# Matmuls on a tile of ones at the start of a cross-attention and gated feed-forward kernel

## The chip, the core and the metric

One core of one Trainium2 chip runs the whole kernel. Five engines work side by side, each through a queue of its own: TensorE (PE) multiplies, VectorE (DVE), ScalarE (ACT) and GpSimd (POOL) do the rest of the arithmetic, and SyncE (SP) issues most DMAs. The metric is device time in microseconds of the whole program; lower is better.

## The reference

The computation is one gated block: cross-attention to a context, then a feed-forward with 4-bit weights. There are 16 batch elements, each with 128 channels and 512 positions, 8 heads of 16 channels, half of them rotated.

```python
def _L0_xattn_ref(x, c, Wq, bq, Wk, bk, Wv, bv, Wo, bo):
    q, k, v = _proj(Wq, bq, x), _proj(Wk, bk, c), _proj(Wv, bv, c)
    # each: (b, 8 heads, 512 positions, 16 channels); rope on the first 8 channels of q and k
    scores = jnp.einsum('bhqd,bhkd->bhqk', q, k) / jnp.sqrt(jnp.float32(kc))
    p_attn = jax.nn.softmax(scores, axis=-1)
    out = jnp.einsum('bhqk,bhkd->bhqd', p_attn, v)
    return _proj(Wo, bo, out)
def _L0_ffn_ref(x, ...):
    gate_up = jnp.einsum('bsh,oh->bso', x, w_gu)      # w_gu, w_down unpacked from 4 bits, scaled
    h = jax.nn.silu(gate) * up
    y = jnp.einsum('bsi,hi->bsh', h, w_down)
    return y / rms
x = x + jnp.tanh(g_xattn[0]) * _L0_xattn_ref(_layernorm(x), ctx_2048, ...)
x = x + jnp.tanh(g_ffn[0]) * _L0_ffn_ref(_layernorm(x), ...)
```

## The kernel before

The kernel is written with queues in an order set by hand: each engine has one list of instructions, and semaphores make it wait for the others. The first part (about 400 us) is the attention over 16 batch elements, the second the feed-forward in four groups.

Batch element `n` goes through these steps. DVE (from `n` = 3 on POOL) normalises its input to `xn`. PE projects q and k, in two halves of the channels, `project_rot` (L788) and `project_pass` (L794), each four instructions. ACT adds the bias (L946). DVE for `n` = 0 and POOL for the others rotate the result and split it into a rounded head and a rest, SP (and ACT once) stores both to an image in DRAM, and SP loads the image back as `qk_stack` in another layout (`load_first` for `n` = 0, `load_half` for the others). Then come the scores. A batch element has 16 slots; `score` (L815) multiplies two heads of one tile of queries into one of two PSUM banks `s_ps`, and DVE takes the maximum of each row out of that bank (`maxima`, L1119). A score waits for the maximum of the score two before it, since the bank is then free. After the eighth and the sixteenth slot `turn_max` (three small DVE operations) turns the maxima, which go through DRAM into two more rows of `qk_stack`. With these rows `weigh` (L827) multiplies the scores again, transposed, ACT takes the exponential, and `values` (L845) multiplies by v.

Batch elements overlap: `tensor_step(b)` has in each slot a score of `b + 1`, the weights of `b`, and the values of `b` from three slots before. In slots 2 and 3 it also has the two halves of the projection of `b + 3`. Ahead of `tensor_step(0)` stands the start of the program: nine matmuls on a tile of ones (`WARM`, L910), the projections of batch elements 0, 1 and 2, and then the 16 scores of batch element 0, with `project_v` (L800) behind slot 3 and two tiny products (L924, L928) behind slots 5 and 6. The image of batch element 0 must be stored and loaded between the projections and these scores.

The change sits in this start, in PE's queue (the function under `@block.tensor`). `v_ones` are the two halves of `v_all`, which DVE fills with ones at the program's start; the later values of v are written into part of them. `pv_ps` is the PSUM bank of the values, `st_ps` are three banks for projections and weights in turn.

Of the kernel before, what the change touches and what calls it, by code (L numbers as in the profile page):

```python
# [17 lines left out]
P = 128  # L18
# [29 lines left out]
ST_BANKS, S_BANKS = 3, 2  # L48
# [4 lines left out]
IMG_ROWS, K_ROW0 = 102, 49  # L53
GROUPS = B // GROUP
FIRST_TURN, TAIL_AT, WARM = 12, 3, 9
BANKS = 4
NT = (B // GROUP) * IT
LAG = 2
# [5 lines left out]
def score_of(slot):  # L64
    return slot // KT, slot % KT
# [8 lines left out]
def transposed_items():  # L74
    items = []
    for n in range(AHEAD_PROJ):
        items += [("rot", n), ("pass", n)]
    items.append(("v", 0))
    for b in range(B):
        for slot in range(SLOTS):  # L80
            if slot == V_AT and b + 1 < B:
                items.append(("v", b + 1))
            items += [("weight", b, 2 * slot), ("weight", b, 2 * slot + 1)]
            if slot == ROT_AT and b + AHEAD_PROJ < B:
                items.append(("rot", b + AHEAD_PROJ))
            if slot == PASS_AT and b + AHEAD_PROJ < B:
                items.append(("pass", b + AHEAD_PROJ))
            if slot == MIX_AT and b >= 2:
                items.append(("mix", b - 2))
    items += [("mix", B - 2), ("mix", B - 1)]  # L90
    return items
# [6 lines left out]
ST_NO = {item: n for n, item in enumerate(transposed_items())}  # L98
# [3 lines left out]
def feed_forward(nc, ctx, d, keep, tiles):  # L102
# [58 lines left out]
    def take_up(dve, T_, k):  # L161
        g, t = divmod(T_, IT)
        at = 4 * T_ + k
        dve.wait_ge(up_done, at + 1)
        bank, out, scale = gu_ps[(2 * k + 1) % BANKS], up[T_ % 2], gu_sc[:, k, IT + t:IT + t + 1]
        if k == 0:
# [146 lines left out]
    def take_gate(act, T_, k):  # L313
        at = 4 * T_ + k
        act.wait_ge(gate_done, at + 1)
        if T_ >= 2:
            act.wait_ge(pairs_ok, 2 * (T_ - 2) + 2)
        nc.scalar.activation(parts[T_ % 2][:, k], gu_ps[(2 * k) % BANKS], ACT.Copy,  # L318
                             scale=gu_sc[:, k, T_ % IT:T_ % IT + 1]).then_inc(gate_read, 1)
# [70 lines left out]
    def gate_up(pe, T_, n):  # L390
# [12 lines left out]
        for moving, first in ((x_head, True), (x_rest, False)):  # L403
            last = nc.tensor.matmul(gu_ps[n % BANKS], gu_vals[:, k, col:col + P], moving[g % 2][:, k],  # L404
                                    start=first, stop=not first)
# [27 lines left out]
def attend(nc, d, keep):  # L433
    with ExitStack() as ctx:
# [28 lines left out]
        v_ones = [v_all[:, p] for p in two]  # L463
# [16 lines left out]
        st_ps = [ps(f"st_ps{r}", [P, T], F32) for r in range(ST_BANKS)]  # L480
        s_ps = [ps(f"s_ps{r}", [P, 2, T], F32) for r in range(S_BANKS)]
        pv_ps = ps("pv_ps", [P, T], F32)
# [15 lines left out]
        values_set = sem("values_set")  # L498
# [14 lines left out]
        st_read = sem("st_read")  # L513
# [59 lines left out]
        with nc.Block() as block:  # L573
# [160 lines left out]
            @block.sync  # L734
            def _(sp):
                load_inputs(sp, 0)
                for out, name in ((wq, "wqT"), (wk, "wkT"), (bias, "qk_bias")):
                    sp.dma_start(out[:], d[name]).then_inc(weights_in, 16)
                for out, name in ((cos, "cos"), (sin, "sin")):
                    sp.dma_start(out[:], d[name]).then_inc(table_in, 16)  # L740
                load_inputs(sp, 1)
                load_inputs(sp, 2)
                load_inputs(sp, 3)
                store_projection(sp, 0, 0)
                store_rest(sp, 0, 1)
                sp.wait_ge(ones_set, 2)
                for j in range(PAIRS):
                    load_first(sp, j)
                for w in two:
                    store_projection(sp, 1, w)  # L750
                store_max(sp, 0, 0)
                load_half(sp, 1, 0)
                load_max(sp, 0, 0)
                for w in two:
                    store_projection(sp, 2, w)
                load_x(sp, 4)
                for b in range(B):
                    sync_step(sp, b)
                gather_sums(sp, B - 1, 1)
                merge_quads(sp, B - 1)  # L760
                sp.wait_ge(pv_done, B * SPANS)
                load_group(sp, 1)
                store_inverse(sp, B - 1)
                load_inverse(sp, B - 1)
                for g in range(GROUPS):
                    ffn["store"](sp, g)
                for stored_p in ffn["stored"]:
                    sp.wait_ge(stored_p, 16 * B // 2)


            def st_bank(pe, item):
                n = ST_NO[item]
                if n >= ST_BANKS:
                    pe.wait_ge(st_read, n - ST_BANKS + 1)
                return st_ps[n % ST_BANKS]

            def s_bank(pe, item):
                n = S_NO[item]
                if n >= S_BANKS:
                    pe.wait_ge(s_read, n - S_BANKS + 1)  # L780
                return s_ps[n % S_BANKS]

            def project_rot(pe, n):
                out = st_bank(pe, ("rot", n))
                pe.wait_ge(normed, n + 1)
                pe.wait_ge(c_in[n % C_TILES], 16 * (n // C_TILES + 1))
                for rows, w, x in ((halves[0], wq, xn), (halves[1], wk, ct[n % C_TILES])):
                    last = nc.tensor.matmul(out[rows], w[:, halves[0]], x[:], start=True, stop=True)  # L788
                last.then_inc(st_full, 1)

            def project_pass(pe, n):
                out = st_bank(pe, ("pass", n))
                for rows, w, x in ((halves[0], wq, xn), (halves[1], wk, ct[n % C_TILES])):
                    last = nc.tensor.matmul(out[rows], w[:, halves[1]], x[:], start=True, stop=True)  # L794
                last.then_inc(st_full, 1)
# [8 lines left out]
            def score(pe, n, slot):  # L804
                j, qt = score_of(slot)
                p = n % 2
                if n == 0:
                    if qt == 0:
                        pe.wait_ge(first_in[j], HALF)
                elif slot % (SLOTS // QUADS) == 0:  # L810
                    pe.wait_ge(half_in[p][j // 2], HALF * ((n + 1) // 2))
                out = s_bank(pe, ("score", n, slot))
                for odd in two:
                    rows = slice(STACK * odd, STACK * odd + DATA_ROWS)
                    last = nc.tensor.matmul(out[:, odd, :], q_stack[p][rows, j, qt * P:(qt + 1) * P], k_stack[p][rows, j, :],  # L815
                                            start=True, stop=True)
                last.then_inc(s_full, 1)
# [87 lines left out]
            @block.tensor  # L905
            def _(pe):
                pe.wait_ge(values_set, 1)
                ones = v_ones[0].rearrange("p k j q c -> p (k j q c)")
                for _ in range(WARM):
                    nc.tensor.matmul(pv_ps[:, 0:P], ones[:, 0:P], ones[:, 0:P], start=True, stop=True)  # L910
                pe.wait_ge(weights_in, WEIGHTS)
                project_rot(pe, 0)
                project_pass(pe, 0)
                for n in (1, 2):
                    project_rot(pe, n)
                    project_pass(pe, n)
                for slot in range(SLOTS):
                    score(pe, 0, slot)
                    if slot == 3:
                        pe.wait_ge(wv_in, 16)  # L920
                        project_v(pe, 0)
                    if slot == 5:
                        pe.wait_ge(wo_in, 16 * 4)
                        nc.tensor.matmul(pv_ps[:, 0:1], wo[:], bias_v[:], start=True, stop=True).then_inc(spread, 1)  # L924
                    if slot == 6:
                        pe.wait_ge(gates_in, 32)
                        pe.wait_ge(consts, 5)
                        nc.tensor.matmul(pv_ps[:, 2:4], ones_row[:], gate_in[:], start=True, stop=True).then_inc(spread, 1)  # L928
                for b in range(B):
                    tensor_step(pe, b)  # L930
                pe.wait_ge(gu_turned, BIT_STEPS)
                for n in two:
                    ffn["gate_up"](pe, 0, n)
                values(pe, B - 1, SPANS - 2, 1)
                for part in two:
                    values(pe, B - 1, SPANS - 1, part)
                for T_ in range(NT + LAG):
                    tensor_feed(pe, T_)
# [409 lines left out]
```

## Time and profile before

| | before |
|---|---|
| time, median of 3 runs | 725.92 us (725.85 to 726.64) |
| profiled execution: time | 726.46 us |
| profiled execution: span of its records | 724.6 us |
| mean granted TensorE clock, share of full | 0.971 |
| PE busy | 692.7 us (96%) |
| DVE busy | 610.9 us (84%) |
| ACT busy | 521.2 us (72%) |
| POOL busy | 476.1 us (66%) |

The span is what the profiler recorded between the first and the last instruction; 1.86 us of the execution's time lie around it. The granted clock is the share of full speed that TensorE was given. It takes two values in this trace, 1.00 (2.4 GHz) and 0.50 (1.2 GHz), and a number between them is a stretch with a switch in it.

### The profile page before, as it was taken

How to read it: one execution, taken by the hardware profiler on the slowest of the kernel's cores; microseconds unless marked ns; L12 is line 12 of the kernel's file. 1: busy time of each engine (PE TensorE's matmuls, PEld its weight loads, DVE VectorE, ACT ScalarE, POOL GpSimd, SP SyncE). 2: the span in 40 equal slices, each digit the busy share in tenths (PEclk: the TensorE clock that was granted, in tenths of full speed). 3: DMA queues.
4: the chain of work that ended last, by engine and by line, in shares of the span. 5: the costliest groups of instructions: out<-in, count | busy, mean ns of one | idle time of the engine just before them, and what ended most of it. 6: DMA issues, size and time to landing. Idle time of an engine off the chain costs nothing.

```text
span 724.6 us, 13389 instructions
## 1 busy us (share of the span) xinstructions
PE 692.7 (96%) x4678; PEld 338.6 (47%) x4678; DVE 610.9 (84%) x825; ACT 521.2 (72%) x925; POOL 476.1 (66%) x403
## 2 busy tenths in 40 slices
PE   3789999999999999999999999999999999999995
PEld 2334434433444344434443444655565556555653
DVE  6698889888988898888889779766899789977894
ACT  1228888888888888888888876665666566666653
POOL 2756655796678667866633129876697669766773
PEclk7659999999999999999999999999999999999998
DMA  7786777687767877877663202000001000100011
GB/s 242 179 207 160 173 197 200 164 186 209 200 167 182 212 191 180 196 200 190 153 160 70 86 24 74 0 1 1 0 1 45 14 1 0 45 16 0 4 42 72
DMA packets 48935, 80.59 MB, mean 111 GB/s; under 512 B 14436, under 2 KB 17892, under 8 KB 48868
## 3 DMA queue, kind: packets, MB, share of 16 engines
q1 hardware_dynamic: 47712, 78.99, 43.0%
q10 hardware_dynamic: 1156, 0.74, 0.4%
q8 instruction: 37, 0.61, 0.4%
q14 instruction: 30, 0.25, 0.1%
HBM read 45.11 MB, written 32.24 MB: 107 GB/s over the span
## 4 chain that ended last, share of the span: by engine, by line
PE 50%; POOL 26%; issue 14%; DVE 4%; DMA 3%; ACT 1%; SPq 1%; POOLq 0%; ACTq 0%; DVEq 0%
PE pv_ps L845 18%; POOL probs L299 15%; PE s_ps L815 14%; POOL probs L303 9%; PE st_ps L827 9%; DVE max_rows L1119 3%; PE st_ps L800 2%; PE st_ps L788 2%; PE st_ps L857 2%; PE st_ps L794 2%; DMA qk_stack<-image 2%; DMA image<-split_head 1%; POOL over_stack L223 1%; DMA inverse_scratch<-sums 1%; PE pv_ps L910 1%
## 5 line engine op out<-in xcount | busy, mean ns | idle before, releaser
L1119 DVE TENSOR_REDUCE max_rows<-s_ps 128x2 f32<-128x1024 f32 x256 | 305.3, 1213 | 42.6 <-PE s_ps L815 41.9
L956 ACT ACTIVATE probs<-st_ps 128x512 f32<-128x512 f32 x512 | 277.5, 595 | 54.0 <-PE st_ps L827 43.7
L318 ACT ACTIVATE probs<-s_ps,gu_sc 128x512 f32<-128x512 f32 x176 | 117.6, 685 | 84.4 <-PE s_ps L404 84.2
L299 POOL TENSOR_TENSOR probs<-probs 128x512 f32<-128x512 f32 x88 | 120.3, 1371 | 69.5 <-ACT probs L318 69.2
L845 PE MATMUL pv_ps<-probs,v_all 128*32 128x256 f32 x2048 | 163.4, 391 | 2.2 <-ACT pv_all L962 2.2
L815 PE MATMUL s_ps<-qk_stack 48*128 48x512 f32 x512 | 132.7, 516 | 7.6 <-DVE max_rows L1119 5.5
L170 DVE SCALAR_TENSOR_TENSOR proj<-s_ps,gu_sc,proj 128x512 f32<-128x512 f32 x132 | 98.8, 749 | 11.1 <-PE s_ps L404 1.9
L827 PE MATMUL st_ps<-qk_stack 50*128 50x512 f32 x512 | 107.9, 411 | 0.0
L420 PE MATMUL st_ps<-dn_head,over_input 128*128 128x512 f32 x264 | 104.8, 423 | 1.0 <-DVE over_input L181 1.0
L815 PEld LDWEIGHTS s_ps<-qk_stack 48*128 48x128 f32 x512 | 49.4, 190 | 114.0 <-issue 70.9
L845 PEld LDWEIGHTS pv_ps<-probs,v_all 128*32 128x32 f32 x2048 | 40.6, 108 | 98.3 <-ACT probs L956 82.3
L1081 POOL TENSOR_TENSOR heads_out<-pv_all,scale_of 128x512 f32<-128x512 f32 x16 | 20.5, 1279 | 92.5 <-DMA scale_of<-inverse_scratch 92.5
L404 PE MATMUL s_ps<-pv_all,gu_bits 128*128 128x512 f16 x352 | 80.1, 380 | 0.2 <-DVE proj L167 0.2
L303 POOL TENSOR_TENSOR probs<-probs 128x512 f32<-128x512 f32 x44 | 71.3, 1621 | 3.4
L404 PE MATMUL s_ps<-split_head,gu_bits 128*128 128x512 f16 x176 | 66.9, 380 | 1.9 <-DVE proj L167 1.5
L827 PEld LDWEIGHTS st_ps<-qk_stack 50*128 50x128 f32 x512 | 63.9, 187 | 8.3 <-issue 3.8
L404 PE MATMUL s_ps<-split_rest,gu_bits 128*128 128x512 f16 x176 | 66.7, 379 | 0.0
L167 DVE TENSOR_SCALAR proj<-s_ps,gu_sc 128x512 f32<-128x512 f32 x44 | 32.9, 747 | 31.7 <-PE s_ps L404 31.7
L1044 POOL TENSOR_TENSOR cross<-proj,sin 128x1024 f32<-128x1024 f32 x15 | 35.8, 2385 | 33.4 <-ACT proj L946 30.8
L420 PEld LDWEIGHTS st_ps<-dn_head,over_input 128*128 128x128 f32 x264 | 49.6, 188 | 17.2 <-ACT over_input L331 1.4
L404 PEld LDWEIGHTS s_ps<-pv_all,gu_bits 128*128 128x128 fp8e3 x352 | 32.1, 98 | 43.4 <-issue 5.9
L420 PE MATMUL st_ps<-dn_rest,over_input 128*128 128x512 f32 x132 | 52.0, 394 | 0.0
(122 smaller groups left out, 891.4 us busy)
## 6 DMA issues: line engine op xcount, KB each, us to landing
qk_stack<-image SPq DMA_DIRECT2D x60, 384.0 KB, 6.2
image<-split_rest SPq DMA_DIRECT2D x32, 256.0 KB
image<-split_head SPq DMA_DIRECT2D x31, 256.0 KB
image<-split_head SPq DMA_DIRECT2D x62, 128.0 KB
xt_all<-x_dram SPq DMA_DIRECT2D x16, 256.0 KB, 3.7
ct<-ctx_dram SPq DMA_DIRECT2D x16, 256.0 KB, 3.5
scale_of<-inverse_scratch SPq DMA_DIRECT2D x16, 256.0 KB
out_dram<-over_stack SPq DMA_DIRECT2D x16, 256.0 KB, 2.0
```

The lines of the kernel that those rows point to most:

```text
L170: nc.vector.scalar_tensor_tensor(out, bank, scale, out, ALU.mult, ALU.add).then_inc(up_read, 1)
L299: nc.gpsimd.tensor_tensor(pair[:, n], parts[T_ % 2][:, 2 * n], parts[T_ % 2][:, 2 * n + 1], ALU.add).then_inc(pairs_ok, 1)
L303: nc.gpsimd.tensor_tensor(gate[T_ % 2], pair[:, 0], pair[:, 1], ALU.add).then_inc(gate_ok, 1)
L318: nc.scalar.activation(parts[T_ % 2][:, k], gu_ps[(2 * k) % BANKS], ACT.Copy, scale=gu_sc[:, k, T_ % IT:T_ % IT + 1]).then_inc(gate_read, 1)
L404: last = nc.tensor.matmul(gu_ps[n % BANKS], gu_vals[:, k, col:col + P], moving[g % 2][:, k], start=first, stop=not first)
L420: last = nc.tensor.matmul(y_ps[j], h[T_ % H_RING][:, cols], keep[w][:, t, :], start=(t == 0 and n == 0), stop=(t == IT - 1 and n == 2))
L815: last = nc.tensor.matmul(out[:, odd, :], q_stack[p][rows, j, qt * P:(qt + 1) * P], k_stack[p][rows, j, :], start=True, stop=True)
L827: nc.tensor.matmul(out[:], k_stack[p][rows, j, kt * P:(kt + 1) * P], q_stack[p][rows, j, :], start=True, stop=True).then_inc(st_full, 1)
L845: last = nc.tensor.matmul(pv_ps[2 * KC * j:2 * KC * (j + 1), cols], v_ones[b % 2][:, kt, j, quad, :], probs[at % PROBS][:, j, cols], start ...
L956: nc.scalar.activation(probs[at % PROBS][:, tile % 4, :], st_ps[item % ST_BANKS][:], ACT.Exp).then_inc(st_read, 1)
L1044: ops.tensor_tensor(cross[:], tile[:], sin[:], ALU.mult).then_inc(crossed, 1)
L1119: nc.vector.tensor_reduce(out, s_ps[item % S_BANKS][:], AXIS_X, ALU.max).then_inc(s_read, 1)
```

## The change

PE gets 38 more matmuls, each of 128 by 128 ones with 192 columns of ones, called `hold`. Nobody reads their results. They read the second half of `v_all`. Twenty stand between the projections of batch elements 0 and 1, five between those of batch element 2 and the first score, and one behind each of the 16 first scores but those of slots 3, 5 and 6. The first 25 write to `pv_ps`, the others to bank 1 of `st_ps`. There are two new waits: for the second tile of ones, and, ahead of the first score, for ACT's reading of the bank that the last 13 write to.

```diff
+HOLD_LONG, HOLD_SHORT, HOLD_COLS = 20, 5, 192
...
                 ones = v_ones[0].rearrange("p k j q c -> p (k j q c)")
+                still = v_ones[1].rearrange("p k j q c -> p (k j q c)")
+
+                def hold(bank):
+                    nc.tensor.matmul(bank[:, 0:HOLD_COLS], still[:, 0:P], still[:, 0:HOLD_COLS], start=True, stop=True)
+
                 for _ in range(WARM):
                     nc.tensor.matmul(pv_ps[:, 0:P], ones[:, 0:P], ones[:, 0:P], start=True, stop=True)
                 pe.wait_ge(weights_in, WEIGHTS)
                 project_rot(pe, 0)
                 project_pass(pe, 0)
+                pe.wait_ge(values_set, 2)
                 for n in (1, 2):
+                    for _ in range(HOLD_LONG if n == 1 else 0):
+                        hold(pv_ps)
                     project_rot(pe, n)
                     project_pass(pe, n)
+                for _ in range(HOLD_SHORT):
+                    hold(pv_ps)
+                pe.wait_ge(st_read, ST_NO["rot", 2] + 1)
                 for slot in range(SLOTS):
                     score(pe, 0, slot)
+                    if slot not in (3, 5, 6):
+                        hold(st_ps[ST_NO["rot", 2] % ST_BANKS])
                     if slot == 3:
```

PE's queue from the last projections (L794) to the scores of slot 5, before the change. The two products of a score are one row each time, and `x8` stands for four scores.

```order
12 L794 MATMUL st_ps<-xn,wq 64x512
13 L794 MATMUL st_ps<-ct,wk 64x512
14 L815 MATMUL s_ps<-qk_stack 128x512 x8
15 L800 MATMUL st_ps<-wv,ct 128x128 x4
16 L815 MATMUL s_ps<-qk_stack 128x512 x4
17 L924 MATMUL pv_ps<-bias_v,wo 128x1
```

The same place after it (lines have moved: L815 is now L816, L800 is L801, and L913 is the new matmul).

```order
14 L795 MATMUL st_ps<-ct,wk 64x512
15 L913 MATMUL pv_ps<-v_all 128x192 x5
16 L816 MATMUL s_ps<-qk_stack 128x512 x2
17 L913 MATMUL st_ps<-v_all 128x192
18 L816 MATMUL s_ps<-qk_stack 128x512 x2
19 L913 MATMUL st_ps<-v_all 128x192
20 L816 MATMUL s_ps<-qk_stack 128x512 x2
21 L913 MATMUL st_ps<-v_all 128x192
22 L816 MATMUL s_ps<-qk_stack 128x512 x2
23 L801 MATMUL st_ps<-wv,ct 128x128 x4
24 L816 MATMUL s_ps<-qk_stack 128x512 x2
25 L913 MATMUL st_ps<-v_all 128x192
```

Five of the new matmuls now stand ahead of the first score and one behind each score but the fourth; nothing else has moved.

PE's queue between the projections of batch element 0 and those of batch element 1, after the change (before it, the rows of L788 followed those of L794 directly).

```order
4 L795 MATMUL st_ps<-xn,wq 64x512
5 L795 MATMUL st_ps<-ct,wk 64x512
6 L913 MATMUL pv_ps<-v_all 128x192 x20
7 L789 MATMUL st_ps<-xn,wq 64x512
8 L789 MATMUL st_ps<-ct,wk 64x512
```

Twenty of the new matmuls stand in front of the projection of batch element 1.

## Rows read from the trace of the kernel before

**Rows 1.** The page: span, PE's busy share and granted clock in tenths, 40 slices.

```profile
span 724.6 us, 13389 instructions
...
PE   3789999999999999999999999999999999999995
...
PEclk7659999999999999999999999999999999999998
```

**Rows 2.** Windows: stretch, length, busy time of each engine, granted clock, DMA share, GB/s.

```profile
10.00:11.00 1.00, 0.00 (x0) 0.00 (x0) 0.94 (x2) 0.00 (x0) 0.00 (x0) 0.92 1.04 395
...
21.00:22.00 1.00, 0.39 (x2) 0.00 (x0) 0.46 (x1) 0.56 (x1) 0.00 (x0) 0.96 0.02 6
...
27.00:28.00 1.00, 0.02 (x2) 0.02 (x2) 1.00 (x2) 0.00 (x0) 0.92 (x2) 0.96 1.11 188
...
36.00:46.00 10.00, 6.36 (x16) 2.38 (x17) 9.90 (x13) 0.00 (x0) 9.41 (x10) 0.50 0.78 193
46.50:55.20 8.70, 8.70 (x32) 2.86 (x29) 6.62 (x12) 5.55 (x10) 0.32 (x1) 0.50 0.87 207
...
55.00:56.00 1.00, 1.00 (x12) 0.30 (x4) 0.00 (x0) 0.53 (x1) 0.39 (x1) 0.89 1.01 139
```

**Rows 3.** Timeline of PE, projections: start, length, line, idle before and its end.

```profile
1.97 4.21 PE L910 MATMUL pv_ps<-v_all 128*128 128x128 f32 x18 [1.97 <-DVE v_all L1178]
...
8.20 0.59 PE L794 MATMUL st_ps<-ct,wk 128*64 128x512 f32 x1
17.88 1.12 PE L788 MATMUL st_ps<-xn,wq 128*64 128x512 f32 x1 [9.09 <-DVE xn L1074]
...
23.54 0.59 PE L794 MATMUL st_ps<-ct,wk 128*64 128x512 f32 x1
26.15 0.73 PE L815 MATMUL s_ps<-qk_stack 48*128 48x512 f32 x4 [2.02 <-DMA qk_stack<-image]
```

**Rows 4.** Timeline of PE, the score of slot 3 and `project_v`.

```profile
29.11 0.80 PE L815 MATMUL s_ps<-qk_stack 48*128 48x512 f32 x2 [0.34 <-DVE max_rows L1119]
29.84 2.07 PE L800 MATMUL st_ps<-wv,ct 128*128 128x128 f32 x8
```

**Rows 5.** Timeline of DVE, the maxima of batch element 0 and later.

```profile
26.70 4.62 DVE L1119 TENSOR_REDUCE max_rows<-s_ps 128x2 f32<-128x1024 f32 x4 [1.86 <-PE s_ps L815]
32.68 4.62 DVE L1119 TENSOR_REDUCE max_rows<-s_ps 128x2 f32<-128x1024 f32 x4 [1.36 <-PE s_ps L815]
...
37.89 9.10 DVE L1119 TENSOR_REDUCE max_rows<-s_ps 128x2 f32<-128x1024 f32 x8
...
56.01 4.93 DVE L1119 TENSOR_REDUCE max_rows<-s_ps 128x2 f32<-128x1024 f32 x4 [1.36 <-PE s_ps L815]
```

**Rows 6.** Timeline of PE: batch element 1's scores of slots 0 and 4.

```profile
46.01 0.80 PE L815 MATMUL s_ps<-qk_stack 48*128 48x512 f32 x2 [0.43 <-DVE max_rows L1119]
46.57 0.66 PE L827 MATMUL st_ps<-qk_stack 50*128 50x512 f32 x2
...
55.47 0.50 PE L815 MATMUL s_ps<-qk_stack 48*128 48x512 f32 x2
```

**Rows 7.** Timeline of PE at full clock: `project_v`, and scores of slots 0, 3, 4.

```profile
64.55 1.16 PE L800 MATMUL st_ps<-wv,ct 128*128 128x128 f32 x8
...
71.58 0.50 PE L815 MATMUL s_ps<-qk_stack 48*128 48x512 f32 x2
...
76.31 0.50 PE L815 MATMUL s_ps<-qk_stack 48*128 48x512 f32 x2
...
78.54 0.50 PE L815 MATMUL s_ps<-qk_stack 48*128 48x512 f32 x2
```

**Rows 8.** Line L612 (`load_half`) between 48 and 56 us: instructions and landings.

```profile
L612 SPq DMA_DIRECT2D qk_stack<-image x2: 422/1094/1767, 49.5 to 49.9; - x2
...
DMA to landing us min/median/max: 5.4/6.3/7.2
```

**Rows 9.** Timeline of POOL: the normalisation of batch element 3.

```profile
46.05 0.77 POOL L1074 TENSOR_SCALAR xn<-xt_all,neg_mean,rstd 128x512 f32<-128x512 f32 x1
```

## The prediction

> **What bounds the kernel now.** I read the page's slices first. PE is busy 9 tenths or more in all slices but the first three and the last, and the granted clock is low in the same first three [rows 1]. So from about 55 us on a chain with PE in it carries the time, and whatever ends earlier at 55 us should end earlier at 724.6 us. The question is what the first 55 us wait for, so I went to the windows and the timelines there.
>
> The granted clock has a history of two drops. It is full up to the first projections, whose last matmul ends at 8.79 us [rows 3], and falls in the window of 10 to 11 us (0.92 there, that is 0.84 us at full and 0.16 at half) [rows 2]. It comes back at 21.1 us (0.96 in the window of 21 to 22), after the projection of batch element 1 has kept PE busy since 17.88 us [rows 2, 3]. It survives PE's idle time of 2.02 us ahead of the first score, but falls at 27.9 us, when PE has had four short products and then idle time again [rows 2, 3]. It then stays at half until 55.2 us, although PE is busy 6.36 of 10 us between 36 and 46 and without a break from 46.5 on [rows 2]. Two things can therefore cost time: the 27.3 us at half from 27.9 to 55.2, and the 10.3 us at half from 10.8 to 21.1.
>
> In each I looked for who waits for PE. From 37.89 us DVE takes eight maxima in 9.10 us without a pause, 1.14 us each [rows 5], while PE needs 0.80 us for a score even at half clock and has 0.34 us idle in a slot [rows 4]. There DVE sets the pace, and a faster PE gives nothing. DVE waits for PE in two places only: 1.36 us ahead of its maxima at 32.68 us [rows 5], when PE has spent 2.07 us on `project_v` [rows 4]; and in `tensor_step(0)`, where PE takes 9.46 us from batch element 1's score of slot 0 (46.01 us) to that of slot 4 (55.47 us) [rows 6] and DVE stands idle 1.36 us once more at the end [rows 5].
>
> The first score itself, at 26.15 us, waits for a DMA, the load of the image [rows 3]. That image comes from batch element 0, whose projections were done at 8.79 us at full clock. The change can't make it come earlier.
>
> **The change, part by part.** A `hold` has no row before. The nearest is the nine matmuls of ones: 18 instructions in 4.21 us at half clock, 0.234 us for 128 columns [rows 3], so 192 columns in two instructions are 0.70 us at half and, if it scales, 0.35 us at full. `project_v` bounds it from above at full clock: 8 instructions of 128 columns in 1.16 us, so 0.29 for two and 0.44 us for a `hold` [rows 7]. I take 0.38 us at full and 0.70 us at half.
>
> The twenty long ones start at about 8.6 us with the clock full, and last 7 to 8.8 us: they end between 15.6 and 17.4 us, ahead of the projection that waits for `xn` until 17.88 us [rows 3]. Their cover is that wait of 9.09 us, so they cost nothing; at half clock they would take 14 us, end at 22.6 us and push everything behind the projection of batch element 1 back by 4.7 us. What they may give is that projection at full clock, some 1.6 us earlier (half of the 3.2 us that it runs at half clock, from 17.88 to 21.1 us [rows 2, 3]). POOL's rotation of batch element 1 then starts earlier. That is worth nothing directly, since the first scores wait for the image of batch element 0, but it brings POOL's later steps forward.
>
> The five short ones end the projection of batch element 2. It ends at 24.13 us now [rows 3], or near 22.5 us. Five times 0.38 is 1.9 us, so they end between 24.4 and 26.0 us, ahead of the load's 26.15: nothing lost, and the idle time there falls from 2.02 us to between 0.1 and 1.8 us. The new wait for ACT's reading of a projection of batch element 2 has its reader done long before 26 us. At half clock five cost 3.5 us and would delay the first score by up to 1.5 us.
>
> The thirteen behind the scores must fit into DVE's 1.14 us. At full clock a slot has about 0.5 us of score and 0.38 us of `hold`, 0.88 us: it fits and costs nothing. What stands behind a `hold` in PE's queue is the next score, which waits for DVE longer than that.
>
> If the clock stays full, two waits go. First, `project_v`: PE starts the score of slot 3 at 29.11 us, `project_v` follows at about 29.5 and takes 1.16 us in place of 2.07 [rows 4, 7], the score of slot 4 is done by 31.2 us, and DVE finishes its four maxima at 31.32 us [rows 5]. DVE no longer waits: **1.36 us** gained, and everything DVE paces until 46.99 us moves forward by it, the score of slot 0 of batch element 1 to 44.65 us. What is late next there is DVE itself.
>
> Second, `tensor_step(0)`. The maxima of batch element 0 then end at 45.63 us (37.89 + 9.10 - 1.36). DVE takes the maximum of slot 0 (1.14), the three small operations of `turn_max` (0.59, from the end of one run of maxima at 37.30 to the next at 37.89 [rows 5]) and the maximum of slot 1 (1.14): 48.5 us, and the score of slot 3 waits for that. From a score of slot 3 to that of slot 4, with a projection half, the weights and the values between them, PE takes 2.23 us at full clock (76.31 to 78.54) [rows 7]. The score of slot 4 comes at 50.7 us, and I add 0.3 us because the projection half may wait for ACT to free a bank: 51.0 against 55.47 us now, **4.4 us** in all, of which 3.1 us are new. Bounds: the whole stretch at full clock, with the previous batch element's values in it, takes 6.96 us (71.58 to 78.54) [rows 7], so at least 9.46 - 6.96 + 1.36 = 3.9 us; if DVE paced nothing, three blocks of values of some 0.6 us would be missing from the 6.96, which gives 5.7 us.
>
> Does anything else hold that point? The projection in slot 2 needs POOL's `xn`, ready at 46.82 us [rows 9] or earlier, and would start near 47.7. The second half of batch element 1's stack is issued at 49.45 us and lands up to 7.2 us later, at 57.0 us [rows 8]; it moves forward with DVE by 1.36 us to 55.7, while the score of slot 8 that reads it comes at 51.0 + 4 slots of about 1.25 = 56.0 us. That is close, but in time.
>
> The profiled execution took 726.46 us, 0.54 us more than the median. 726.46 - 4.4 is 722.1 us, and against the median it is 721.5 us. I say 721.6.
>
> A rule of the Trainium skill would make this safer than the rows do. "TensorE: Matmul & The Clock Gate", in its section on why this matters for a kernel, asks for no idle gaps above about 3 us between bursts of matmuls. By that the gaps left here (under 3 us) all keep the clock, and the full 4.4 us come. This trace doesn't agree: the clock fell 2.1 us after the last matmul at 8.79 us, and at 27.9 us with no gap above 2.02 us. So I keep a chance for the clock to fall.
>
> **The rivals.** (B) The clock falls in the idle time before the first score or among the first scores, and comes back while they run. For it: the drop at 27.9 us. Against: PE is then far busier than it was. With the clock at half a slot needs 0.56 us of score (46.01 to 46.57) [rows 6] and 0.70 of `hold`, 1.26 us against DVE's 1.14. Four such slots cost 0.5 us and `project_v`'s 1.36 us stays; 3.1 - 0.5 = 2.6 us gained, 723.3 us.
>
> (C) The load of batch element 1's second half comes late. If the issue or the landing doesn't move forward at all, slot 8 starts at 57.0 and not at 56.0 us, and the maximum rows of batch element 0 that follow it in SP's queue may be later still: 1 to 2 us lost, 723.1 us.
>
> (D) **Slower.** The clock falls near 26 us and stays down until 55 us, as it does now with PE busy without a break from 46.5 us. Then the `hold`s are in the way: 1.26 us a slot (1.5 us by the score's full 0.80 us) in place of 1.14, thirteen times: 1.6 to 4.7 us. It decides where score and `hold` together pass 1.14 us, which at half clock they do. 727.5 us at the least, I take 728.
>
> (E) The clock falls as before but the `hold`s hide in PE's idle 0.34 us and the idle at the ends: 725.9 us.
>
> **How the numbers follow.** The forecast (A) gets 54 in 100, B 16, C 7, E 7, D 16. D is not small because a busy PE alone did not bring the clock back between 46.5 and 55.2 us. The time is that of A, 721.6 us; its own range is 720.3 (the 5.7 us) to 722.4 us. The range of 8 in 10 leaves out D and the edges of A: 720.6 to 726.3 us. A measurement of this kernel can tell 0.2%, 1.45 us, from no change. A, B and C lie beyond it, less a little of B and C: faster 0.75. E and the rest: same 0.09. D: slower 0.16.
>
> **What would show it.** Right: a granted clock of 1.00 in all windows between 27 and 55 us; DVE without the 1.36 us of idle time near 31 us; the score of slot 4 of batch element 1 near 51 us; the same 4.4 us less at the end. A `hold` of 0.35 to 0.44 us. Wrong: half clock in the windows of 28 to 46 us with DVE waiting for PE in every slot (D), or a wait for a DMA ahead of the score of slot 8 (C). If the first score is later than 26.2 us, the long or short `hold`s have overrun their cover.

## The result and the profile after

The changed kernel takes 730.24 us (median of 6, 728.47 to 732.85) against 725.88 us (median of 6, 725.44 to 726.64): ratio 1.0063, 95% interval 1.0039 to 1.0087. It is slower. Rival D happened, the forecast didn't. All comparisons leave out executions that took over 1.5% more than the fastest of their kernel, which only two kernels below have (four of 12 and three of nine). The changed kernel's executions differ by up to 4.4 us, and the longer ones have the lower mean granted clock (0.976 at 732.85 us, 0.981 at 728.47); the kernel before stayed within 1.2 us.

The page of the changed kernel, its span, PE's busy share and the granted clock in 40 slices. The profiled execution took 732.85 us.

```profile
span 731.0 us, 13542 instructions
...
PE   7899999999999999999999998999999999999996
...
PEclk9758999999999999999999999999999999999999
```

The first slices show more clock than in [rows 1], the third and fourth (36 to 73 us) still 5 and 8. The windows tell when it fell.

```profile
25.00:26.00 1.00, 0.46 (x3) 0.24 (x3) 0.00 (x0) 0.00 (x0) 1.00 (x1) 1.00 1.06 217
26.00:27.00 1.00, 1.00 (x6) 0.56 (x4) 0.91 (x1) 0.00 (x0) 0.85 (x3) 0.62 1.06 227
...
36.00:46.00 10.00, 10.00 (x27) 4.81 (x25) 8.28 (x10) 0.17 (x1) 8.01 (x10) 0.50 0.49 85
...
60.00:61.00 1.00, 1.00 (x12) 0.21 (x10) 0.34 (x2) 0.50 (x1) 0.00 (x0) 0.81 1.01 131
```

The clock was full to 26.2 us (0.62 in that window), so up to there it was kept, through the twenty and the five `hold`s. It then stood at half until about 60.4 us: 34 us, where [rows 2] had 27. PE is busy for 10.00 of 10 us between 36 and 46, where [rows 2] had 6.36, and DVE for 8.28, where it had 9.90. DVE no longer sets the pace.

The timeline of PE (start, length, line, operation; L913 is the `hold`, L816 the score).

```profile
8.04 6.77 PE L913 MATMUL pv_ps<-v_all 128*128 128x192 f32 x40
17.20 0.64 PE L789 MATMUL st_ps<-xn,wq 128*64 128x512 f32 x1 [2.40 <-DVE xn L1088]
...
21.80 1.89 PE L913 MATMUL pv_ps<-v_all 128*128 128x192 f32 x10
25.55 0.50 PE L816 MATMUL s_ps<-qk_stack 48*128 48x512 f32 x2 [1.85 <-DMA qk_stack<-image]
...
40.20 0.79 PE L816 MATMUL s_ps<-qk_stack 48*128 48x512 f32 x2
40.92 1.00 PE L913 MATMUL st_ps<-v_all 128*128 128x192 f32 x2
41.86 0.79 PE L816 MATMUL s_ps<-qk_stack 48*128 48x512 f32 x2
...
51.82 0.79 PE L816 MATMUL s_ps<-qk_stack 48*128 48x512 f32 x2
...
60.95 0.50 PE L816 MATMUL s_ps<-qk_stack 48*128 48x512 f32 x2
```

A slot with a `hold` takes 1.66 us at half clock (40.20 to 41.86): 0.72 us from the score's start to the `hold`'s, and 0.94 us from there to the next score. DVE waits in each of them, as its own timeline shows.

```profile
42.70 1.23 DVE L1133 TENSOR_REDUCE max_rows<-s_ps 128x2 f32<-128x1024 f32 x1 [0.43 <-PE s_ps L816]
44.36 1.23 DVE L1133 TENSOR_REDUCE max_rows<-s_ps 128x2 f32<-128x1024 f32 x1 [0.43 <-PE s_ps L816]
```

The account between the two profiled executions: the first score starts at 25.55 in place of 26.15 us (-0.60). From it to batch element 1's score of slot 0 PE takes 26.27 us in place of 19.86 (+6.41): twelve slots at 1.66 in place of 1.14 are 6.2 us. From slot 0 to slot 4 it takes 9.13 in place of 9.46 us (-0.33). That is +5.48 us at the score of slot 4 (60.95 against 55.47, [rows 6]). It is +5.51 us at the last score of the attention (410.06 against 404.55 us), so nothing more is lost or won in between. The span grew by 6.4 us. The other 0.9 us arose in one place of the feed-forward, where PE waited for DVE for 2.14 in place of 1.29 us (timelines of PE, the kernel before and the changed one):

```profile
441.26 0.39 PE L404 MATMUL s_ps<-split_head,gu_bits 128*128 128x512 f16 x1 [1.29 <-DVE proj L167]
```

```profile
447.63 0.39 PE L405 MATMUL s_ps<-split_head,gu_bits 128*128 128x512 f16 x1 [2.14 <-DVE proj L168]
```

Why it is longer is open. Of the profiles of the experiments, three lose 0.2 to 0.5 us against the kernel before in the same stretch (427 to 445 us), and eight less than 0.05 us.

### The profile page after: what moved, and what is told of

It reads as the page before. It is cut to its first block, busy times and chain, and to the rows that moved or that the text cites. A ratio compares the mean times of both kernels' runs of the same rounds, so it can differ in the third digit from the quotient of the medians.

```text
span 731.0 us, 13542 instructions
## 1 busy us (share of the span) xinstructions
PE 710.8 (97%) x4754; PEld 353.0 (48%) x4754; DVE 611.7 (84%) x825; ACT 521.3 (71%) x925; POOL 475.7 (65%) x403
## 4 chain that ended last, share of the span: by engine, by line
PE 56%; POOL 26%; issue 13%; DVE 1%; DMA 1%; ACT 1%; POOLq 0%; ACTq 0%; DVEq 0%; SPq 0%
PE pv_ps L846 20%; PE s_ps L816 16%; POOL probs L300 15%; PE st_ps L828 9%; POOL probs L304 9%; PE st_ps L801 3%; PE st_ps L789 2%; PE st_ps L858 2%; PE st_ps L795 2%; PE st_ps L913 2%; DMA image<-split_head 1%; POOL over_stack L224 1%; PE pv_ps L916 1%; DMA qk_stack<-image 1%; ACT probs L970 0%
## 5 line engine op out<-in xcount | busy, mean ns | idle before, releaser
L816 PE MATMUL s_ps<-qk_stack 48*128 48x512 f32 x512 | 133.7, 518 | 1.8 <-DMA qk_stack<-image 1.8
L816 PEld LDWEIGHTS s_ps<-qk_stack 48*128 48x128 f32 x512 | 49.6, 190 | 107.0 <-issue 75.1
```

## The experiments

Theory H: the loss is the thirteen `hold`s behind the scores, run at half clock. The rival S puts it ahead of the scores. The other theories ask why the clock falls. G, G2, G3 and G4 name single places where PE stands idle or has little to do, one more with each number; W says that a score with 192 columns is too little in every slot. The first four kernels were measured on one chip against 25 executions of the kernel before, median 725.48 us.

### Without the thirteen behind the scores

```diff
-                    if slot not in (3, 5, 6):
-                        hold(st_ps[ST_NO["rot", 2] % ST_BANKS])
```

> Keeps the twenty and the five matmuls of ones ahead of the scores and takes out the thirteen behind the scores. Theory H (the loss is the thirteen at half clock, 1.66 us a slot against DVE's 1.14): the loss goes, 725.5 us, and the granted clock still falls near the first scores. Rival S (the loss is made ahead of the scores, by the twenty or the five): still about 730 us. Rival F (the matmuls ahead keep the clock up by themselves): 721 to 723 us.

Measured: 725.11 us (11 executions, 724.6 to 725.89), ratio 0.9996, interval 0.9987 to 1.0004. The loss is gone and nothing is gained. In its timeline: DVE's maxima, SP's issues of the maxima's store (L627) and of `load_half` (L613), and batch element 1's first score.

```profile
26.35 9.14 DVE L1131 TENSOR_REDUCE max_rows<-s_ps 128x2 f32<-128x1024 f32 x8 [1.58 <-PE s_ps L816]
...
36.20 0.52 SPq L627 DMA_DIRECT2D max_scratch<-max_lines  x1
37.95 0.79 SPq L613 DMA_DIRECT2D qk_stack<-image  x2
...
45.01 0.80 PE L816 MATMUL s_ps<-qk_stack 48*128 48x512 f32 x2 [1.23 <-DMA qk_stack<-image]
```

Its windows over the scores (columns as in [rows 2]):

```profile
26.00:34.00 8.00, 5.18 (x28) 2.79 (x26) 7.65 (x7) 0.77 (x2) 7.63 (x8) 1.00 0.78 194
34.00:35.00 1.00, 0.49 (x2) 0.22 (x2) 1.00 (x2) 0.00 (x0) 1.00 (x1) 0.86 0.83 244
```

The clock was full from 26 to 34.7 us without any `hold` among the scores, and DVE took eight maxima without a pause: the 1.36 us of `project_v` were gained. Then batch element 1's first score waited 1.23 us for its load. SP had stored the maxima 1.80 us earlier than before, but issued the load only 0.67 us earlier than the 38.62 us it had; ahead of it stand only the waits for the stores of that image. In this execution the projection of batch element 1 ran at half clock (it fell at 17.6 us), so its image was no earlier. That is rival C, at another load than the one I looked at. The second gain stayed out because the clock was at half again from 34.7 to 55.2 us: from slot 0 to slot 4 of `tensor_step(0)` PE took 9.57 us, where it had 9.46.

### Only the thirteen behind the scores

```diff
-HOLD_LONG, HOLD_SHORT, HOLD_COLS = 20, 5, 192
+HOLD_LONG, HOLD_SHORT, HOLD_COLS = 0, 0, 192
```

> Keeps the thirteen matmuls of ones behind the scores and takes out the twenty and the five ahead of them. Theory H: the clock falls as it did before the change, near 28 us, and every slot behind it takes 1.66 us: 730 us or a little more. Rival S: 726 us. If a half clock comes back under the denser work, about 728 us.

Measured: 728.58 us (8 executions), ratio 1.0047, interval 1.0031 to 1.0062. Theory H stands and S falls: the thirteen alone make a loss. In the profiled execution the clock happened to rise at 27 us, after long projections at half, and fell again at 33.8 us, so that only slot 0 and the slots from 7 on were slow.

```profile
33.00:34.00 1.00, 0.69 (x4) 0.31 (x4) 1.00 (x2) 0.17 (x1) 1.00 (x2) 0.89 0.76 246
```

### Ten ahead of the first score

```diff
-HOLD_LONG, HOLD_SHORT, HOLD_COLS = 20, 5, 192
+HOLD_LONG, HOLD_SHORT, HOLD_COLS = 20, 10, 192
```

> Ten in place of five matmuls of ones ahead of the first score, so that they last until about 25.4 us and PE has almost no idle time before the first score. Theory G (the clock falls because of the idle time of about 2 us ahead of the first score): the granted clock is 1.00 through the scores, no slot takes more than 1.2 us, and the time is 721 to 723 us. Rival W (the scores with their matmuls of ones are too little work to keep it): it falls some us later and the time is 728 to 730 us. If the ten are run at half clock they delay the first score by up to 3 us: 732 us.

Measured: 728.19 us (5 executions), ratio 1.0041, interval 1.0028 to 1.0053. Timeline of PE at full clock, and the same two operations at half.

```profile
26.40 0.51 PE L816 MATMUL s_ps<-qk_stack 48*128 48x512 f32 x2
26.83 0.59 PE L913 MATMUL st_ps<-v_all 128*128 128x192 f32 x2
27.36 0.50 PE L816 MATMUL s_ps<-qk_stack 48*128 48x512 f32 x2
...
36.08 0.79 PE L816 MATMUL s_ps<-qk_stack 48*128 48x512 f32 x2
36.81 1.01 PE L913 MATMUL st_ps<-v_all 128*128 128x192 f32 x2
37.74 0.79 PE L816 MATMUL s_ps<-qk_stack 48*128 48x512 f32 x2
```

The window in which the clock fell:

```profile
33.00:34.00 1.00, 1.00 (x4) 0.61 (x4) 1.00 (x2) 0.00 (x0) 1.00 (x1) 0.57 0.52 139
```

With the idle time ahead of the first score filled, the clock stayed full over the first seven slots. A slot's work is 0.96 us there, below DVE's 1.14, so a `hold` costs nothing at full clock. It fell at 33.1 us (0.57 in that window; the next expectations say 33.6), behind slots 5 and 6, which have none. G named a place, but not the only one.

### The same with 64 columns behind the scores

```diff
-                        hold(st_ps[ST_NO["rot", 2] % ST_BANKS])
+                        hold(st_ps[ST_NO["rot", 2] % ST_BANKS], 64)
```

> As the run with ten, with the thirteen matmuls of ones behind the scores cut from 192 to 64 columns. If the price of one at half clock goes by its columns, it is 0.43 us less (128 columns of 4 passes at 1.2 GHz) and a slot takes 1.23 us at half: 726.5 us if the clock falls, and 722 us if it stays. If it goes by the loading of weights and the change between kinds of matmul, a slot stays above 1.5 us at half.

Measured: 726.21 us (12 executions, 725.44 to 729.91), ratio 1.0019, interval 1.0007 to 1.0031. A slot at half clock takes 1.34 us:

```profile
41.88 0.79 PE L816 MATMUL s_ps<-qk_stack 48*128 48x512 f32 x2
42.60 0.69 PE L913 MATMUL st_ps<-v_all 128*128 128x64 f32 x2
43.22 0.79 PE L816 MATMUL s_ps<-qk_stack 48*128 48x512 f32 x2
```

Cutting 128 of 192 columns took 0.32 us off the 0.94; in proportion it would have been 0.63. Carried on to no columns (an estimate), 0.46 us of a `hold` at half clock have nothing to do with its columns. The 0.72 us ahead of it did not change. Both ends of my expectation for a slot, 1.23 and above 1.5 us, missed; the time came near the 726.5 us.

### One behind slots 5 and 6 too

The next three kernels and their 29 executions of the kernel before (median 726.14 us) shared a chip. The first has ten ahead of the first score and 15 behind the scores; the second makes these 256 columns; the third has the 15 of 192 columns, and five ahead as in the changed kernel.

```diff
-                    if slot not in (3, 5, 6):
+                    if slot != 3:
```

> As the run with ten ahead of the first score, and with a matmul of ones behind the scores of slots 5 and 6 too, 15 in all. In the run with ten the clock was full for the first seven slots (0.95 us a slot, no loss) and fell at 33.6 us, after slots 4 to 7, of which two have none. Theory G2 (two weak places: the idle time ahead of the scores, and slots 5 and 6): the clock stays full to the end of the scores and through tensor_step(0), 721 to 723 us. Rival W (a score and 192 columns a slot are too little): it falls within the scores again, a few us later, 726 to 729 us.

> As the run with 15, with 256 columns each. At full clock a slot's work is about 1.06 us against DVE's 1.14, so it costs nothing there. If the columns decide whether the clock stays (Rival W): 721 to 723 us here and not with 192. If both stay full: the same time in both. If it falls in both, this one is slower by 0.2 us for each slot at half.

> The changed kernel with a matmul of ones behind the scores of slots 5 and 6 too, and five ahead of the first score as in it. Theory G2: the idle time of about 1.9 us ahead of the first score still brings the clock down in some executions and not in others, so the times spread from 722 to 732 us, and the median lies above that of the run with ten. If slots 5 and 6 were the only weak place: 721 to 723 us.

Measured: with 192 columns 727.32 us (12 executions, 722.61 to 728.48), ratio 1.0007, interval 0.9993 to 1.0021. With 256 columns 723.42 us (12, 721.99 to 726.84), ratio 0.9980, interval 0.9962 to 0.9997: the first that is faster than the kernel before. Seven of its executions took 721.99 to 723.71 us with a mean clock of 0.996 or more, five 726.39 to 726.84 us with 0.990. With 192 columns and five ahead the ratio is 1.0004 (0.9986 to 1.0022), from eight executions between 721.33 us (mean clock 0.997) and 728.07 us (0.988). The other four took 732.66 to 736.06 us, with a mean clock of 0.972 to 0.976, no higher than the changed kernel's (0.976 to 0.982). The time goes with the clock. The median of all 12 is 727.75 us, above the 727.32 us with ten, as G2 forecast, but by too little to show it; that none of the 12 with ten took over 728.48 us speaks for G2 more.

Slots 5 and 6 are a weak place: with `hold`s behind them the ratio is 1.0007 in place of 1.0041, and in its profile the clock no longer fell there. It fell at a third place. In the profile with 192 columns and ten ahead, the row of PE's timeline behind DVE's `turn_max`, and from its windows the one in which the clock fell:

```profile
37.05 0.50 PE L816 MATMUL s_ps<-qk_stack 48*128 48x512 f32 x2 [0.76 <-DVE max_rows L1133]
```

```profile
39.00:41.00 2.00, 1.79 (x8) 0.76 (x6) 2.00 (x3) 0.00 (x0) 2.00 (x2) 0.63 1.05 180
```

In the profile with five ahead it fell in the same stretch, at about 38.4 us. That profile says nothing on the idle time ahead of the first score, which was short in it:

```profile
26.48 0.51 PE L816 MATMUL s_ps<-qk_stack 48*128 48x512 f32 x2 [0.28 <-DMA qk_stack<-image]
```

The clock had fallen at 18.0 us already, in PE's 2.39 us of idle time ahead of the projection of batch element 1; that projection ran at half clock, and everything behind it came later. So whether the clock falls at the first place decides how much idle time is left at the second (0.28 us here, 1.85 us in the changed kernel, with the same five ahead). With 256 columns seven of 12 executions took under 724 us, with 192 one of 12, which is what W forecast of these two kernels; five of 12 fell short even with 256.

### Two behind slot 9, then 26 ahead of the projection, then none ahead of the scores

All three keep 256 columns behind the scores; the kernel before took 725.83 us beside them (20 executions).

```diff
-                        hold(st_ps[ST_NO["rot", 2] % ST_BANKS], 256)
+                        for _ in range(2 if slot == 9 else 1):
+                            hold(st_ps[ST_NO["rot", 2] % ST_BANKS], 256)
```
```diff
-HOLD_LONG, HOLD_SHORT, HOLD_COLS = 20, 10, 192
+HOLD_LONG, HOLD_SHORT, HOLD_COLS = 26, 10, 192
```
```diff
-HOLD_LONG, HOLD_SHORT, HOLD_COLS = 26, 10, 192
+HOLD_LONG, HOLD_SHORT, HOLD_COLS = 26, 0, 192
```

> As the run with 15 of 256 columns, with two of them behind the score of slot 9, where PE stands idle because DVE does its three small operations (0.76 us of idle time in the run with 192 columns, and the clock fell behind it there and in the run with five ahead). Theory G3 (this idle time is the third weak place): nearly all executions have a mean clock of 0.99 or more and take 722 to 724 us; the 726.5 us of 5 in 12 executions are gone. Rival: the 726.5 us come from another place, and as many are left.

> As the run with two behind slot 9, with 26 in place of 20 ahead of the projection of batch element 1, which then end at about 17 us and leave nearly no idle time there. The clock fell at 17.8 us in the profiles of two runs. If this matters: fewer executions at half clock in the projections, first image stored earlier, 722 us. If not: the same time as with 20. If one of the 26 is late, the projection starts later: some tenths slower.

> As the run with 26, with none ahead of the first score, so that the 4 us of idle time there are back, while the scores have all their matmuls of ones. Theory G (this idle time is a weak place by itself): the clock falls in many executions before or with the first score, each slot behind it then takes 1.8 us at half, 731 us or more; with none falling there, 722 us. Rival (the idle time is harmless when the scores are dense): as the run with 26.

Measured: two behind slot 9, 723.71 us (12 executions), ratio 0.9984, interval 0.9968 to 1.0001. Four of 12 took above 726 us, where five of 12 did: G3 is not shown. With 26 ahead of the projection, 723.09 us (5 executions), ratio 0.9956, interval 0.9943 to 0.9969; the plain mean of the five, one of which took 725.85 us, gives 0.9966. With none ahead of the first score, ratio 1.0045, interval 1.0022 to 1.0068, from six executions of 725.11 to 732.38 us; the other three took 738.39, 738.85 and 837.64 us, and the median of all nine is 731.62 us, as G forecast. The idle time there is a weak place by itself, also where the scores are dense. Its effect is the largest of all edits here, 0.9956 against 1.0045. It is read from the times alone: the execution that was profiled is the one of 837.64 us, in which the granted clock was 0.75 from 6 us on, and it doesn't show where the clock falls in the others.

The idle time behind the twenty is a weak place too. In four of the eight profiles with twenty the clock fell in the 2.4 us of idle time ahead of the projection of batch element 1 (at 17.6 to 18.4 us), in none of the three with 26. Where it fell and ten stood ahead of the first score (two profiles), these ten ended late and the first score started at 27.6 us, where it started at 25.5 to 26.1 us in the three others with twenty and ten. Fillers that were priced at full clock overran their cover there, by some 1.5 us.

In the profile with 26, the projection of batch element 1 follows at once (a row of PE's timeline), and the clock fell in `tensor_step(0)` (a window):

```profile
17.87 0.64 PE L789 MATMUL st_ps<-xn,wq 128*64 128x512 f32 x1 [0.44 <-DVE xn L1089]
```

```profile
47.00:49.00 2.00, 1.60 (x10) 0.69 (x9) 1.93 (x5) 1.81 (x4) 0.00 (x0) 0.85 0.86 299
```

### The kernel with 26 again, and with two more in `tensor_step(0)`

The two new waits keep PE's write behind the last reading of the same bank by DVE and by ACT.

```diff
                     weigh(pe, b, slot)
+                    if b == 0 and slot < 2:
+                        pe.wait_ge(gated, 1)
+                        pe.wait_ge(consts, 6)
+                        still = v_ones[1].rearrange("p k j q c -> p (k j q c)")
+                        nc.tensor.matmul(pv_ps[:, 256:448], still[:, 0:P], still[:, 0:192], start=True, stop=True)
```

> The same kernel as the run with 26, measured again beside the run before it in this list and the kernel before on one chip. It should repeat the ratio of 0.9956, with most executions between 721.8 and 723.5 us and some above 725 us where the clock fell near 48 us.

> As the run with 26, ten, and 15 of 256 columns, and one matmul of ones of 192 columns behind the weights of slots 0 and 1 of tensor_step(0), each after waits for DVE's and ACT's last reading of the bank that it writes (DVE's reading ends at about 46.0 us, when the first of them would start). PE stands idle 0.3 and 0.4 us there for DVE, and the clock fell at 48.3 us in the profile of one run with 26. Theory G4 (this is the fourth weak place): no execution above 724 us, 722.5 to 723.5 us. Rival: as in the run with 26, with one in five executions above 725 us. If the waits hold PE up, some tenths slower.

Measured: the kernel with 26 again 723.36 us (5 executions, 722.39 to 723.56), ratio 0.9958, interval 0.9945 to 0.9972, a repeat. With the two more, 722.97 us (6 executions, 722.58 to 723.26) against 726.06, ratio 0.9959, interval 0.9947 to 0.9972. The two can't be told apart by their times, since the kernel with 26 had no execution above 723.6 us this time. For G4 speaks that in the profile with 26 the clock fell again at 48.2 us (until 51.6 us), and in the one with two more not before 719 us; one profile of each does not settle it. Both beat the kernel before, and the changed one by their ratios. The last one's profile is what I had forecast for the change. Its windows:

```profile
27.00:36.00 9.00, 9.00 (x42) 5.02 (x40) 8.73 (x10) 0.77 (x2) 8.70 (x7) 1.00 0.93 241
36.00:46.00 10.00, 9.28 (x37) 4.43 (x36) 9.97 (x12) 0.86 (x2) 8.41 (x10) 1.00 0.79 190
46.00:56.00 10.00, 9.79 (x75) 3.82 (x74) 9.35 (x14) 8.17 (x15) 3.91 (x2) 1.00 0.91 213
```

The scores of slots 0 and 4 in its timeline of PE:

```profile
44.41 0.50 PE L816 MATMUL s_ps<-qk_stack 48*128 48x512 f32 x2
...
51.60 0.50 PE L816 MATMUL s_ps<-qk_stack 48*128 48x512 f32 x2
```

The clock is full to 56 us, DVE is busy for 9.97 of 10 us from 36 to 46, and the score of slot 4 starts at 51.60 us, 3.9 us earlier than in [rows 6]. Of these, 0.5 us stand already at the first score (25.62 against 26.15 us), whose start moves from 25.5 to 26.7 us between the profiles with the clock full there; 1.1 us come in the scores and 2.3 us in `tensor_step(0)`.

## Why the prediction was wrong

The step that failed is the condition on which the sum stood, "If the clock stays full, two waits go". I gave it 54 in 100 from rows that spoke against it: the clock had fallen at 27.9 us with no idle time above 2.02 us ahead of it, and it had stayed at half for 8.7 us under a PE without a pause. I took the reduced idle time for enough. Instead the clock fell at 26.2 us, behind the 1.85 us of idle time left ahead of the first score, and stood at half for 34 us; twelve slots of 1.66 in place of 1.14 us made the loss, and both waits stayed. That the `hold`s behind the scores are the loss is shown (0.9996 without them, 1.0047 with them alone). That the 1.85 us brought the clock down is supported, not shown: with ten and no idle time there the same scores ran at full clock to 33.1 us in the one profile of that kernel, and with none there the ratio rose from 0.9956 to 1.0045. Slots 5 and 6 are a second place (the clock fell behind them at 33.1 us, and at 33.8 us with the thirteen alone).

Point by point:

- **What waits for PE** was right. The two places of DVE's waiting are where a full clock gave the time back. In the last kernel 3.9 us were gained by the score of slot 4, where I had 4.4 with a lower bound of 3.9; by the medians it is 3.1 us of 726.06. Part of this agreement is luck: 0.5 us of it is the earlier first score, which the forecast did not count. `project_v` and the scores gave 1.1 us, where I had 1.36, and `tensor_step(0)` 2.3, where I had 3.1. The stretch from slot 0 to slot 4 took 7.19 us, where I had added up 6.35.
- **The twenty and the five** cost nothing, as forecast: 6.77 us for twenty (0.34 each; I had 0.38), and 1.89 for five. By themselves they give nothing either (ratio 0.9996).
- **A `hold` at full clock** costs nothing behind a score, as forecast: 0.96 us a slot, where I had 0.88. The `hold` itself takes 0.53 us there, above the 0.44 us that I had taken for an upper bound from `project_v`.
- **A `hold` at half clock** was the mis-sized term of rival D. I had 1.26 us a slot, or 1.5 at most; it is 1.66. The row of nine matmuls of ones in a row gave 0.70 us for it, but between two scores it takes 0.94, and the score ahead of it 0.72 in place of 0.56. (The prediction calls the clock full up to the first projections and yet prices these nine at half clock. The price is the right one: the windows give 1.00 there only because the trace holds no record of the clock before 7.4 us, 5.8 us in the changed kernel, and twenty `hold`s at full clock took 0.17 us an instruction for 192 columns, where the nine took 0.23 us for 128.) So D's 728 us was 2.2 us too low, and the 730.24 us lie outside a range that was cut at 726.3 to leave D out.
- **The rivals.** D was named with its place, its price and the point from which it decides, and got 16 in 100. Rival B (the clock comes back among the scores) did not happen in any profile in which it fell there: it stayed down until the projection halves of `tensor_step(0)`. C happened at the load of batch element 1's first half, and cost 1.23 us in the one profile without `hold`s among the scores, in which the projection before it ran at half clock.
- **The rule of the Trainium skill** on idle gaps above about 3 us, which would have made the forecast safe, is contradicted again: in the changed kernel the longest idle time of PE between 2 and 26 us was 2.40 us, and the clock fell at 26.2 us behind 1.85 us. The page "TensorE: Matmul & The Clock Gate" of the Trainium skill has the other side as well, in its section on a second failure mode: in a bf16 kernel that cycled through PSUM banks, frequent short idle times between groups of matmuls made the clock go down and up. These runs agree that short idle times are no protection. Without the thirteen PE stood idle six times among the scores, for 0.25 to 1.09 us, and the clock fell at 34.7 us; with 15 of 192 columns and ten ahead it stood idle for 0.76 and 0.20 us, and the clock fell at about 39.5 us.

Open stay three things: why PE waited 0.9 us longer for DVE near 447 us in the changed kernel's profile; whether 26 `hold`s ahead of the projection do better than 20 (above 725 us took one of ten executions, against five of 12, which ten executions can't tell from chance); and whether the last two `hold`s in `tensor_step(0)` do anything. What decides in one execution whether the clock falls was not tried, and most places where it fell rest on one profile each.

## What to carry to other kernels

Work that is put in to hold a clock must be priced at the clock it is meant to prevent: here it is free at full clock (0.96 us under DVE's 1.14) and costs 0.52 us a slot at half (1.66 against 1.14). Close every place where the engine still stands idle, and look at the spread of the executions beside the median: the kernel with 20, ten, and 15 of 256 columns took 722 to 724 us in seven of its 12 executions and 726.4 to 726.8 us in the other five. If not all of them can be closed, putting filler only where nobody waits for the engine (the run without the thirteen) at least loses nothing.

## What the runs showed of the hardware

- At half clock PE was busy without a break from 26.7 to 60.4 us in the changed kernel, scores and matmuls of ones in turn, and the clock did not return in between; it did so at 60.4 us, at the end of the second of the two projection halves in slots 2 and 3.
- A matmul of 192 columns in two instructions took 0.34 us in a row of twenty and 0.53 us between scores at full clock, and 0.94 us between scores at half: there the price doesn't scale with the columns alone.
- At full clock without any matmuls of ones among the scores the clock held for 8.7 us, with PE busy 5.18 of 8 us.
- The granted clock had a third value in one execution: 0.75 from 6 us to the end, in that of 837.64 us, of a program on one core. No other profile has it, and nothing in the runs says why.
- Ahead of the projection of batch element 1 the clock fell in 2.4 us of idle time in four of eight profiles, and in none of three where 0.4 us of it were left.
